# Transposes ahead of score matmuls on TensorE, and key rounding one unit earlier on ScalarE, in a fused attention and expert kernel

## The reference, cut to what matters

```python
scores = jnp.einsum('bhqd,bhkd->bhqk', Q, K) / np.sqrt(dh)
x = lax.conv_general_dilated(scores.transpose(0, 2, 1, 3).reshape(b * s, h, s), conv_w,
                             window_strides=(1,), padding=[(1, 1)], dimension_numbers=('NCW', 'OIW', 'NCW'))
scores = (x + conv_b[None, :, None]).reshape(b, s, h, s).transpose(0, 2, 1, 3)
weights = jax.nn.softmax(scores, axis=-1)
out = jnp.einsum('bhqk,bhkd->bqhd', weights, V).reshape(b, s, e)
return out @ Wo.T + bo
```

## Time and profile before

| | value |
|---|---|
| median of the runs | 263.09 us |
| profiled execution, its own time | 265.03 us |
| its span, first to last instruction | 263.1 us |
| mean granted TensorE clock | 0.983 |
| busy: TensorE / VectorE / ScalarE / GpSimd | 91% / 79% / 64% / 54% |
| attention, from the first maximum to the last O | about 26 to 217 us |
| S(n): three matmuls of 128x512, x124 | 465 + 397 + 398 ns (they overlap) |
| maximum, x128 / exponential, x128 | 738 / 719 ns |
| `kc` on VectorE, x31 | 1080 ns mean |
| `ta` / `tc_` / `td` / `Kl` on GpSimd | 983 / 813 / 1329 / 1292 ns |

### The profile page before, as it was taken

How to read it: one execution, slowest core, us unless ns; L and a number is a source line. 1 busy time by engine, 2 the same in 40 slices (tenths; PEclk the granted TensorE clock), 3 DMA queues, 4 the chain that set the end, 5 groups by cost and what they waited for, 6 DMA issues and landing times.

```text
span 263.1 us, 5532 instructions
## 1 busy us (share of the span) xinstructions
PE 239.2 (91%) x1775; PEld 186.7 (71%) x1775; DVE 209.1 (79%) x509; ACT 168.5 (64%) x307; POOL 143.0 (54%) x166
## 2 busy tenths in 40 slices
PE   7996978989898998999999879799998999999993
PEld 7454856867676776867877757578777876879982
DVE  1549899888979889897987998979979666677553
ACT  2643589967778687787868557778679660214321
POOL 1019779978679787787968446779783000000000
PEclk9999879999999999999999999999999999999998
DMA  6950007456273535637353507163544704400002
GB/s 206 360 232 0 0 4 220 144 120 189 51 226 133 120 122 118 198 99 182 125 120 123 118 31 210 59 183 123 120 165 120 196 4 125 197 0 2 0 2 80
DMA packets 13766, 31.73 MB, mean 121 GB/s; under 512 B 1458, under 2 KB 10674, under 8 KB 13490
## 3 DMA queue, kind: packets, MB, share of 16 engines
q1 hardware_dynamic: 13314, 30.82, 38.9%
q10 hardware_dynamic: 432, 0.65, 0.8%
HBM read 19.14 MB, written 12.32 MB: 120 GB/s over the span
## 4 chain that ended last, share of the span: by engine, by line
PE 62%; DVE 14%; issue 9%; ACT 6%; POOL 4%; DMA 2%; DVEq 1%; SPq 0%; ACTq 0%; POOLq 0%
PE sc L829 8%; PE tp L974 8%; PE sc L831 6%; PE sc L830 6%; PE pvbank L850 6%; PE pvbank L848 5%; DVE Pb L554 5%; PE sc L1060 3%; PE tp L1070 3%; DVE w2s L689 2%; ACT Kh L354 2%; POOL Kl L256 2%; ACT Pb L359 2%; DVE kc L498 2%; PE sc L1020 1%
## 5 line engine op out<-in xcount | busy, mean ns | idle before, releaser
L359 ACT ACTIVATE Pb<-Pb,nbias 128x512 f32<-128x512 f32 x128 | 90.9, 719 | 42.2 <-DVE Pb L554 41.0
L554 DVE TENSOR_SCALAR_CACHE_REDUCE Pb<-sc,col 128x512 f32<-128x512 f32 x128 | 92.0, 738 | 15.1 <-PE sc L831 13.9
L829 PE MATMUL sc<-Kh,Ql 128*128 128x512 f32 x124 | 57.6, 465 | 9.0 <-issue 4.6
L256 POOL TENSOR_TENSOR Kl<-kc,Kh 128x512 fp32r<-128x512 f32 x29 | 37.5, 1292 | 31.0 <-ACT Kh L354 30.3
L974 PE MATMUL tp<-cst,Pb 128*128 128x128 f32 x332 | 50.3, 275 | 4.1 <-ACT PT L406 4.0
L974 PEld LDWEIGHTS tp<-cst,Pb 128*128 128x128 f32 x332 | 40.5, 141 | 17.4 <-issue 4.9
L831 PE MATMUL sc<-Kh,Qh 128*128 128x512 f32 x124 | 49.3, 398 | 0.0
L830 PE MATMUL sc<-Kl,Qh 128*128 128x512 f32 x124 | 49.3, 397 | 0.0
L406 ACT ACTIVATE PT<-tp 128x512 f32<-128x512 f32 x79 | 46.0, 582 | 1.2 <-PE tp L974 1.2
L268 POOL TENSOR_TENSOR td<-ta,tc_ 128x512 f32<-128x512 f32 x31 | 41.2, 1329 | 2.6
L261 POOL TENSOR_SCALAR ta<-Kp,cwS 128x512 f32<-128x512 f32 x31 | 30.5, 983 | 16.0 <-ACT Kp L332 15.9
(11 more groups left out here) (241 smaller groups left out, 305.7 us busy)
## 6 DMA issues: line engine op xcount, KB each, us to landing
swap<-w2s SPq DMA_DIRECT2D x15, 768.0 KB, 3.3
PT<-swap SPq DMA_DIRECT2D x60, 192.0 KB, 3.9
w1s<-in_w SPq DMA_DIRECT2D x1, 2048.0 KB, 10.6
w2s<-in_w SPq DMA_DIRECT2D x1, 2048.0 KB, 7.9
cst<-in_consts SPq DMA_DIRECT2D x1, 648.0 KB, 6.2
xTs<-in_xT SPq DMA_DIRECT2D x2, 256.0 KB, 3.5
we<-in_wexp SPq DMA_DIRECT2D x2, 256.0 KB, 4.0
b2s<-in_b2row SPq DMA_DIRECT2D x1, 512.0 KB, 11.4
```

The lines of the kernel that those rows point to most:

```text
L256: pool.tensor_tensor(Kl[:, n, :], kc[:, n, :], Kh[:, n, :].bitcast(f32), ALU.subtract)\
L359: act.activation(Pb[:, k, :], Pb[:, k, :], ACT.Exp, bias=nbias[:, k:k + 1], scale=-1.0)\
L554: dve.tensor_scalar(Pb[:, k, :], SC[k % 4][:, :], cb, None, ALU.subtract, ALU.min, accum_out=nbias[:, k:k + 1]).then_inc(s["mx"], 1)
L829: pe.matmul(SC[k][:, :], ql, Kh[:, h2, :], start=True, stop=False)
```

## The change

TensorE: within a unit, T(n) is issued ahead of S(n+4). ScalarE: `high_half` moves from the unit at position 0 of a head, where it followed the first exponential of a head, to the unit at position 3 of the head before, where it follows the fourth exponential (the exponentials run four units ahead); it rounds the same heads, each one unit earlier. The third head's rounding is called once ahead of the loops, behind the first four exponentials.

```diff
                 if not isinstance(g, int) or n + AHEAD < U * NG * B:
                     exp(n + AHEAD, (u + AHEAD) % RING)
-                if u % QT == 0 and (not isinstance(g, int) or hd + 2 < B * H):
-                    high_half(hd + 2, (u // QT) % 2)
+                if u % QT == 3 and (not isinstance(g, int) or hd + 3 < B * H):
+                    high_half(hd + 3, (u // QT + 1) % 2)
                 if u == 9:
                     stage_values(b, g)
 
             for k in range(AHEAD):
                 exp(k, k)
+            high_half(2, 0)
             for u in range(TURN):
...
                 gi = NG * b + g
                 n, m = U * gi + u, u + AHEAD
-                if not isinstance(g, int) or n + AHEAD < U * NG * B:
-                    over = isinstance(g, int) and G * g + m // QT >= H
-                    scores(n + AHEAD, H * b + G * g + m // QT, b + 1 if over else b, m)
                 if not by_blocks(b, g, u):
                     pe.wait_ge(s["ex"], n + 2)
...
                     mm.then_inc(s["tpx" if last_pair(b, g, u) and u % 2 == 0 else "tp"], 1)
+                if not isinstance(g, int) or n + AHEAD < U * NG * B:
+                    over = isinstance(g, int) and G * g + m // QT >= H
+                    scores(n + AHEAD, H * b + G * g + m // QT, b + 1 if over else b, m)
```

## The result

The changed kernel takes 274.96 us (median of four runs, 272.5 to 275.78); the kernel before, run beside it, 263.18 us (262.97 to 263.51). By the medians it is 11.8 us slower; the ratio is 1.041, with an interval of 1.037 to 1.045 (9.6 to 11.9 us). Ratios leave out the slow runs, those over 1.5% above the fastest of the same kernel, and medians hold all. The forecast had the sign and the mechanism of the swap, and 271.0 us for the size; the measured median lies 0.5 us above its range.

What follows compares the result with a forecast made beforehand. The prediction took a loop over all engines (O, first score, VectorE's queue, ScalarE's exponential and eviction, T(7), O) to set each half's length; 8.6 us less 0.7 gave 7.9, so 263.09 + 7.9 = 271.0 us, range 264.5 to 274.5.

Steps and rivals of the forecast that it cites:

- Part 1 (b): End of a half: S(11) stands between waiting T(7) and O; eviction to O 1.94 us, +0.73 or +0.68 a half.
- the sum: Two kinds of half at 4.1 us each, last half 0.4: together 8.6; less 0.7 estimated elsewhere: 7.9 us.
- Part 1 (a): Inside a half: T(n) 0.78 us earlier, S(n+4) 0.36 later; VectorE has a backlog there, so nothing.
- (c), the last half: Last half: its first unit puts a transpose (0.36) ahead of the score VectorE waits for: +0.4 us.
- Part 2 (b): Kh moves between the fourth and fifth exponential and stays on the ScalarE chain; eviction at 94.83 for 94.87: -0.04 us.
- Part 2 (c): 11.00 us halves: earlier Kl puts GpSimd's `td` under VectorE's `kc`, +0.38 us; eviction +0.14.
- The three halves of batch 0: Halves carrying batch 0's stages are full of other work, so T(7) finds its eviction done: 0.
- the clock, taken as full: TensorE's clock read as full (1.00); a half at 11.99 us busy was taken to show room.
- The rival: Clock falls once in each of ten halves as TensorE idles more: +8.5 us on top, 279.5 us; chance 0.04.
- What I said would show it: Signs: longer O to O, eviction waits over 12 us, Kl and Kh waits a third, VectorE's score waits some 8 more.
- GpSimd's wait for Kh: Sign for the early Kh: GpSimd's waits for Kh shrink to a third.

Runs made afterwards that it cites:

- swap alone: Kernel before with only T(n) issued ahead of S(n+4), Kh where it was: 271.68 us, ratio 1.032.
- swap in unit 7 alone: Kernel before with T(7) ahead of S(11) in the last unit of each half only, Kh as before: 272.02 us, ratio 1.031.
- Kh alone: Kernel before with only the key rounding moved one unit earlier, S(n+4) still ahead of T(n): 266.08 us, ratio 1.006.
- the fillers: Changed kernel plus matmuls with unused results: five ahead of each waiting T(7), ten in the first half, nine ahead of `diag`: 271.26 us, ratio 1.027.
- odd heads' Kh alone: Kernel before with only the odd heads' key rounding moved earlier: 265.51 us, ratio 1.007.
- the other swaps stand beside the early Kh: Changed kernel with S(11) ahead of T(7) again in the last unit of each half: 268.16 us, ratio 1.016.

## Why the prediction was right, and where it was not
**Part 1 (b), the score between T(7) and O: right, in mechanism and size.** Forecast 1.94 us from eviction to O; measured 1.91, as 0.62 to T, 0.41 for T and 0.88 for the score with the change to O. The whole swap was put at 7.8 and 0.4; alone it measured 8.3, though not in the places of the sum (0.96 of it stands in halves 7 to 10), and its place at unit 7 alone gives the ordinary halves whole. A waiting T(7) held back a ready S(11) at both places shown: program order, as the page "TensorE: Matmul & The Clock Gate" of the Trainium skill (section "Step-by-step: what each phase is for") has it.

**Part 1 (a), inside a half: right.** The swaps in the other units cost nothing in ordinary halves. **(c), the last half, +0.4: right** (10.76 to 11.13, and 10.75 where only unit 7 is swapped).

**Part 2 (b), the chain through ScalarE, -0.04: right in the half shown.** The eviction comes 10.37 us after O where it was 10.42, and the half of 11.63 became 12.28: +0.70 - 0.05 = +0.65, as measured. Halves 2, 6 and 12 grew by less, 0.56, 0.47 and 0.48, where the forecast had 0.69 for each; why is not shown.

**Part 2 (c), the collision of `kc` with `td`: mis-sized.** `kc` did begin 6.25 us after O, but O itself came later, and GpSimd was earlier than I placed it. In the half from 101.37:

```profile
107.62 0.82 DVE L499 SCALAR_TENSOR_TENSOR kc<-Kp,col,td 128x512 f32<-128x512 f32 x1
```

```profile
106.58 1.31 POOL L268 TENSOR_TENSOR td<-ta,tc_ 128x512 f32<-128x512 f32 x1
...
110.53 1.27 POOL L256 TENSOR_TENSOR Kl<-kc,Kh 128x512 fp32r<-128x512 f32 x1 [2.04 <-ACT Kh L354]
```

`td` ends 0.27 us into `kc`, which loses 0.06, not 0.38. The eviction comes 9.54 after O for 9.74: -0.20 in place of +0.14, and the half grew by 0.65 - 0.20 = 0.45 (11.00 to 11.45), not 0.82. The collision is real, and shows whole where Kh is early and O isn't late (1.49, Kh alone). The five halves of this kind (1, 3, 5, 11 and 13) grew by 0.45 to 0.70, 2.8 together, not 4.1. Of these, halves 1, 3 and 5 took 0.68 to 0.70 more with the swap alone, where the forecast had 0.68; the early Kh beside it then took 0.2 off, where the forecast had 0.14 on top.

**The three halves of batch 0 at nothing: wrong.** Halves 7 to 10 grew by 0.96 with the swap alone at full clock, 0.70 of it in half 10 and 0.36 in half 9. T(7) does wait in some of these. The other way, the ten halves outside (1 to 6, 11 to 14) grew by 5.3 in the changed kernel, where the forecast's terms for them are 4 x 0.69 + 5 x 0.82 + 0.4 = 7.3. So the sum was put together from terms too small and too large, and its nearness to 271.26, the time with the fillers, is in part luck: less the fillers' own 1.4 us, the changed kernel at full clock would take some 269.9, 6 to 7 us above the kernel before (an estimate; 263.7 ran beside it, 263.18 beside the changed kernel), where the sum was 7.9.

**The step that failed is the clock, taken as full.** The sum has no term for it. The changed kernel was granted 0.978 to 0.991 in its four runs, 272.5 us at 0.991 and 275.3 and 275.78 at 0.978 and 0.981. The rival had 0.04, and foresaw a fall in each of ten halves. In the ordinary halves the clock did stay, as the forecast had it, with 10.1 us busy of 11.45. It falls where TensorE idles longest in one piece: ahead of the first Kl (2.17), ahead of T(7) in the first half (2.71) and ahead of `diag` in the stages of batch 0 (2.39). I had looked only at the ordinary halves. By the medians the kernel with the fillers is 3.7 us faster; with the fillers' own 1.4 the falls cost about 5 us in the changed kernel (an estimate). Of that the change itself is shown to bring the fall at `diag`, 1.8 us in half 10. The fall at 24.5 us comes with the same wait before and after, so it isn't the change's, and whether the next one is stays open. The median of before hardly holds any (262.97 to 263.51 beside the changed kernel; its runs at full clock took 262.8 to 263.9). The swap alone keeps the clock in three of four runs; with the early Kh beside it the wait for `diag` is longer (1.67 to 2.39), as with odd heads' Kh alone (2.41). With Kh alone the clock fell there behind a wait of only 1.82, while the swap in unit 7 alone has one of 1.82 too, ahead of T(7) in half 10, with no fall, so the length of the wait doesn't decide alone.

**What I said would show it.** O to O at 11.45 and 12.28 for 11.8 and 12.2; the waits for evictions over 12 (17.7); the waits of TensorE for Kl gone. VectorE's wait for scores grew by 11.0 for 8; with the swap alone at full clock by 6.1. GpSimd's wait for Kh should have shrunk to a third and grew from 27.7 to 39.4, by 11.7, about what the whole run grew: GpSimd's busy time hardly changes (143.0 and 138.8), and a longer half only adds to its idle time. That expectation named no step of the sum, but was worked out carelessly: an earlier Kh moves the idle time of an engine that isn't the bound, and can't remove it.

**Open.** Why the clock falls at 24.5 us in some executions and not in others behind the same wait, and how much of the wait of 2.71, and of the fall behind it, is a result of that first fall (the swap alone, without it, has 1.76 there and no fall); what makes `diag` later when odd heads' Kh is early; and where the half of 16.2 us comes from when the other swaps stand beside the early Kh. The executions of one kernel also differ by more than the clock: that of before ran in 265.19 us at 0.994 and in 263.16 at 0.996.

## What to carry to other kernels
In a queue that keeps its order, put behind an instruction that will wait only what can wait as long; a ready one belongs ahead of it, and the price of the wrong order is most of its length at each place where the wait ends the loop (0.70 of 0.88 us in some eleven places here). Look for long single waits of TensorE outside the ordinary loop too, and ask which of them the change lengthens: the clock fell behind two of 2.4 to 2.7 us, and the one at `diag` cost 1.8 us in the half behind it. And moving an operation by one unit moves every collision behind it, so judge it by both positions in the loop, not by the one it leaves.

## What the runs showed of the hardware
Adding 178 passes of matmuls of ones, 0.13 us each (ten in 1.27), went with a granted clock of 0.999 or 1.000 in all four runs and 3.7 us less time; in the half behind `diag` it took 1.8 us off.

Behind the first O, in all fourteen traces, the clock fell behind each of the ten waits of TensorE of 1.99 to 2.58 us, and behind one of 1.82, while it held behind another of 1.82 and behind all shorter ones. Ahead of the first O, behind the wait for the first Kl of 2.17, it fell in six traces and held in eight. The kernel before spreads by 2 us: 263.0 at 1.00, 265.2 at 0.983, but 265.2 at 0.994 too.

A `kc` of VectorE takes 0.70 to 0.71 us where GpSimd does nothing beside it. Begun inside a `td` or `Kl` of GpSimd that had 0.20 us or more to go, it ended 0.53 to 0.56 us after that instruction in all 210 cases of the fourteen traces, whether it had lain beside it for 0.2 or for 1.3 us (0.75 to 1.85 us in all): beyond the first 0.16 or so, time inside the other instruction did nothing for it. It goes the other way round too: eight `kc` that began 0.04 to 0.06 us ahead of a `td` took 0.74, and the `td` took 1.81 to 1.84 in place of 1.30. In the changed kernel:

```profile
164.63 0.74 DVE L499 SCALAR_TENSOR_TENSOR kc<-Kp,col,td 128x512 f32<-128x512 f32 x1
```

```profile
164.67 1.83 POOL L268 TENSOR_TENSOR td<-ta,tc_ 128x512 f32<-128x512 f32 x1
```

So the one that begins first holds the other up, and what a collision costs `kc` is how long the GpSimd instruction still has to run, less some 0.16 us: 0.27 us to go cost 0.11, and 0.94 cost 0.78.
